# Expert blocks of a four-layer attention and feed-forward kernel: gathers placed ahead of accumulating stores, first gathers and weights issued during routing, router logits in four column tiles of 32

## The reference

```
x = x + cross_attention_0(layernorm(x), ctx)
x = x + moe_0(layernorm(x))            # 8 experts, top 2, F = 704
x = x + feature_map_attention_1(ctx, ctx, layernorm(x))
x = x + block_1(layernorm(x))          # latent attention, then MoE: 7 experts of F = 256 and a shared one
x = x + nearest_context_row(layernorm(x), ctx)
x = x + fp4_feed_forward_2(layernorm(x))
x = x + cross_attention_3(layernorm(x), ctx)
x = x + moe_3(layernorm(x))            # 8 experts, top 2, F = 512

moe: probs = softmax(x @ router_w); top 2 of 8, weights normalised
     out[token] = sum over its 2 experts of w * (silu(x @ Wg[e]) * (x @ Wu[e])) @ Wd[e]
```

## Time and profile before

| | us |
|---|---|
| median of 3 runs | 1805.71 (1800.82 to 1808.09) |
| profiled execution, its own time | 1800.69 |
| its span | 1798.8 |
| stages e0n to the first gate product of e0b | 133.2 to 188.4 |
| blocks of e0b, first to last rows turned | 187.5 to 476.0 |
| stages e3n to the first gate product of e3b | 1474.3 to 1525.5 |
| blocks of e3b, first to last rows turned | 1524.6 to 1769.9 |
| PE busy | 1550.2 (86%) |
| POOL busy | 486.0 (27%) |
| mean granted TensorE clock | 0.946 |

### The profile page before, as it was taken

The page is one execution under the profiler, slowest core; times in us unless marked ns, Lnnn a source line. Parts: engine busy times, 40 slices in busy tenths (PEclk is TensorE's granted clock), DMA queues, the critical chain, the costliest instruction groups (busy, mean ns, idle before and its releaser), DMA issues. The chain is left out here.

```text
span 1798.8 us, 33336 instructions
## 1 busy us (share of the span) xinstructions
PE 1550.2 (86%) x11830; PEld 1155.5 (64%) x11831; DVE 958.4 (53%) x2462; ACT 487.2 (27%) x1029; POOL 486.0 (27%) x594
## 2 busy tenths in 40 slices
PE   5887999999979986999979899578897888988885
PEld 3653899999858742455444566346665654878785
DVE  4455244444359866766556333689885464222221
ACT  2331111011067531455621122223322431000000
POOL 0101344444400001111102343422120102455543
PEclk9998999999969998999999999788998998999998
DMA  4108677777510017244115133200000025666665
GB/s 142 40 8 277 221 226 223 218 212 222 154 50 2 2 36 194 61 108 111 52 32 170 50 88 82 62 24 13 1 1 1 2 62 189 206 200 201 200 182 140
DMA packets 128641, 200.84 MB, mean 112 GB/s; under 512 B 20368, under 2 KB 77968, under 8 KB 128336
## 3 DMA queue, kind: packets, MB, share of 16 engines
q1 hardware_dynamic: 107696, 169.65, 29.3%
q0 software_dynamic: 20832, 29.68, 8.4%
HBM read 166.21 MB, written 35.16 MB: 112 GB/s over the span
## 5 line engine op out<-in xcount | busy, mean ns | idle before, releaser
L1528 DVE TENSOR_REDUCE l1a_nm<-l1a_sc 128x1 f32<-128x512 f32 (+3 forms) x256 | 107.1, 482 | 53.7 <-PE l1a_sc L1664 53.7
L2271 PEld LDWEIGHTS e0b_gp<-e0b_xT,e0b_wgu 128*128 128x128 f32 x936 | 110.5, 192 | 4.2 <-issue 1.5
L2271 PE MATMUL e0b_gp<-e0b_xT,e0b_wgu 128*128 128x128 f32 x936 | 111.0, 275 | 1.9 <-DVE e0b_hT L2350 1.4
L2331 ACT ACTIVATE e0b_sg<-e0b_gp 128x640 f32<-128x640 f32 x78 | 33.5, 481 | 270.9 <-PE e0b_gp L2271 270.9
L2242 POOL DMA_INDIRECT y_sum<-e0b_yb,e_token x39 | 63.5, 1628 | 145.6 <-DVE e0b_yb L2358 142.5
L2271 PE MATMUL e0b_up<-e0b_xT,e0b_wgu 128*128 128x128 f32 x780 | 93.5, 275 | 0.0
L2242 POOL DMA_INDIRECT y_sum<-e3b_yb,e_token x39 | 63.0, 1617 | 102.2 <-DVE e3b_yb L2358 99.3
L2271 PEld LDWEIGHTS e0b_up<-e0b_xT,e0b_wgu 128*128 128x128 f32 x780 | 90.2, 192 | 0.0
L2331 ACT ACTIVATE e3b_sg<-e3b_gp 128x512 f32<-128x512 f32 x39 | 23.3, 597 | 236.2 <-PE e3b_gp L2271 236.2
L2271 PE MATMUL e3b_up<-e3b_xT,e3b_wgu 128*128 128x128 f32 x624 | 80.3, 285 | 0.0
L2271 PEld LDWEIGHTS e3b_gp<-e3b_xT,e3b_wgu 128*128 128x128 f32 x624 | 75.6, 192 | 3.5 <-issue 0.9
(11 more groups left out here) (619 smaller groups left out, 3755.9 us busy)
## 6 DMA issues: line engine op xcount, KB each, us to landing
e3b_wgu<-in_L_ffn_W SPq DMA_DIRECT2D x78, 512.0 KB, 4.6
e0b_wgu<-in_L_ffn_gate_proj SPq DMA_DIRECT2D x39, 704.0 KB, 4.3
e0b_wgu<-in_L_ffn_up_proj SPq DMA_DIRECT2D x39, 704.0 KB, 5.6
x_rows<-xn SPq DMA_DIRECT2D x3, 2048.0 KB, 8.6
l_parts<-l1p_split SPq DMA_DIRECT2D x16, 384.0 KB, 3.1
l_stack_k<-l_parts SPq DMA_DIRECT2D x48, 128.0 KB, 2.7
l_stack_q<-l_parts SPq DMA_DIRECT2D x48, 128.0 KB, 3.0
y_slots<-e1b_yb SPq DMA_DIRECT2D x38, 128.0 KB
```

Source lines behind the costliest of these rows:

```text
L1528: nc.vector.tensor_reduce(nm[:, g % 2, q, i:i + 1], sc[q], AX_X, ALU.max, negate=True).then_inc(max_done, 1)
L2271: last = nc.tensor.matmul(dst[:, f, :], wgu[j][:, k, at + f * P:at + (f + 1) * P], xT[j][:, k, :], start=(k == 0), stop=(k == KC - 1))
L2331: last = nc.scalar.activation(sg[rows, chunks, :], gp[rows, chunks, :], ACT.Silu)
```

## The change

It moves instructions on POOL, SP, PE, ACT and DVE and adds few.

1. **POOL's order in blocks**: `send` and `fetch_weight` stand one block later, behind `fetch(n)`: `send(n - 4)`, `fetch_weight(n - 2)`.
2. **Issued during route** (e0, e3): gathers of blocks 0 and 1 (POOL, at the end of route, once `token` is made) and the gate and up weights of block 0 (SP, once `owner` is made). The dummy matmuls at the opening of blocks go from 30 to 4; 16 are added at the end of route.
3. **Memory of the down projections in e0**: the last pieces (those with the half-filled chunk that POOL must clear) now go to `xnT`, so the clearing waits for nothing; the others go to `xn`, once its store has landed.
4. **Router logits**: the router columns are padded with zeros to 32; each of the four token tiles of a batch is made in a column tile of its own (32 stationary columns, 128 moving), so `lt` is 128 by 128, and one transpose turns a batch.
5. **a1**: four groups of four tiles; the first group's statistics stand ahead of the value bias additions on DVE; one Sqrt and one Exp table load fewer.

```diff
@@ normalise @@
-                lt = [st.enter_context(nc.psum_tensor(f"{tag}_lt{j}", [E, S], F32)) for j in range(2)]
-                lts = st.enter_context(nc.sbuf_tensor(f"{tag}_lts", [E, B, S], F32))
+                lt = [st.enter_context(nc.psum_tensor(f"{tag}_lt{j}", [P, P], F32)) for j in range(2)]
+                lts = st.enter_context(nc.sbuf_tensor(f"{tag}_lts", [P, B, P], F32))
...
                         for k in range(KC):
-                            last = nc.tensor.matmul(lt[b % 2][:], wr[:, k, :], xnT[:, k, b * S:(b + 1) * S],
-                                                    start=(k == 0), stop=(k == KC - 1))
+                            for t in range(TB):
+                                at = (b * TB + t) * P
+                                last = nc.tensor.matmul(lt[b % 2][t * ROUTER:(t + 1) * ROUTER, :], wr[:, k, :], xnT[:, k, at:at + P],
+                                                        start=(k == 0), stop=(k == KC - 1))
...
                         pe.wait_ge(lt_copied, b + 1)
-                        for t in range(TB):
-                            nc.tensor.transpose(lp[:, b * TB + t, 0:E], lts[:, b, t * P:(t + 1) * P], ident[0:E, 0:E])
+                        nc.tensor.transpose(lp[:, b * TB:(b + 1) * TB, :].rearrange("p t e -> p (t e)"), lts[:, b, :], ident)
@@ feature_attention @@
-        GROUPS = [(0, 2), (2, 4)] + [(b * TB, (b + 1) * TB) for b in range(1, B)]
+        GROUPS = [(b * TB, (b + 1) * TB) for b in range(B)]
...
                     copy_rows(0)
-                    roots(1)
                     act.preload_act_table(ACT.Exp)
@@ SummedBlocks @@
-            homes = [inner, xnT, xn]
+            homes = [inner, xn, xnT] if self.FC > 4 else [inner, xnT]
...
+        def load_gate_up(self, sp, owner, n, j):
+            e = sp.value_load(owner[0:1, bass.ds(n, 1)], min_val=0, max_val=self.E - 1)
+            for at, m in ((0, self.w_gate), (self.F, self.w_up)):
+                sp.dma_start(self.wgu[j][:, :, at:at + self.F], m[e].rearrange("(k p) f -> p k f", p=P)).then_inc(self.gu_in[j], 16)
@@ route @@
                     last.then_inc(token_made, 1)
+                    if plan is not None:
+                        stay_busy(idle[:], 16)
...
                     if plan is not None:
-                        for dst, source in plan.late[0]:
+                        if plan.LEFT:
+                            sp.dma_start(x_rows[T * P:, :].rearrange("(t p) d -> p t d", p=P), xn[:, 0:2, :]).then_inc(sent, 16)
+                            sp.wait_ge(left_cleared, 1)
+                        for dst, source in plan.late[-1]:
                             sp.dma_start(dst, source).then_inc(plan.kept, 16)
-                        if len(plan.late) > 1:
-                            sp.dma_start(x_rows[T * P:, :].rearrange("(t p) d -> p t d", p=P), xn[:, 0:2, :]).then_inc(sent, 16)
+                        sp.wait_ge(step, 20)
+                        plan.load_gate_up(sp, owner, 0, 0)
+                        if plan.LEFT:
                             sp.wait_ge(sent, 32)
-                            sp.wait_ge(left_cleared, 1)
-                            for dst, source in plan.late[1]:
+                            for dst, source in plan.late[0]:
                                 sp.dma_start(dst, source).then_inc(plan.kept, 16)
...
                     if plan is not None and plan.LEFT:
-                        pool.wait_ge(sent, 32)
                         plan.clear_left(left_cleared)
...
+                    if plan is not None:
+                        pool.wait_ge(routed, 2)
+                        pool.wait_ge(sent, 32 if plan.LEFT else 16)
+                        for n in range(2):
+                            pool.indirect_dma_start(plan.xb[n][:], None, x_rows, bass.IndirectOffsetOnAxis(ap=token[:, n:n + 1], axis=0))\
+                                .then_inc(rows_in[n], 16)
@@ blocks @@
-                    load_gate_up(0, 0)
-                    load_gate_up(1, 1)
+                    plan.load_gate_up(sp, owner, 1, 1)
...
-                    fetch(0)
-                    fetch(1)
                     fetch_weight(0)
                     fetch_weight(1)
                     pool.wait_ge(plan.start_written, 16 * len(plan.start))
                     for n in range(2, NB):
                         fetch(n)
-                        if n >= 3:
-                            send(n - 3)
-                            fetch_weight(n - 1)
-                    send(NB - 3)
-                    fetch_weight(NB - 1)
-                    send(NB - 2)
-                    send(NB - 1)
+                        if n >= 4:
+                            send(n - 4)
+                            fetch_weight(n - 2)
+                    for n in range(NB - 4, NB):
+                        send(n)
+                        if n + 2 < NB:
+                            fetch_weight(n + 2)
...
-                    stay_busy(gp[:, 0:4, :].rearrange("p f c -> p (f c)"), 30)
+                    stay_busy(gp[:, 0:4, :].rearrange("p f c -> p (f c)"), 4)
```

More of the change, by code:

```diff
@@ L262, in _ @@
                     sp.dma_start(dst, src).then_inc(weights_loaded[0], 16)
+            @block.gpsimd
+            def _(pool):
+                for router in w.router:
+                    nc.gpsimd.memset(router[:], 0.0).then_inc(cleared, 1)
+                pool.wait_ge(cleared, len(w.router))
             @block.vector
@@ L856, in _ @@
                     split_bias()
-                    for b in range(B):
+                    for t in range(TB):
+                        count(t)
+                    for t in range(TB):
+                        aggregate(t)
+                    for b in range(2):
                         dve.wait_ge(v_made, b // 2 * 2 + 2)
```

77 lines of the change are left out of this document (39 added, 38 removed).

## The result

| | before | changed |
|---|---|---|
| median, us | 1803.26 (1799.31 to 1808.09, 4 runs) | 1744.36 (1742.65 to 1747.71, 4 runs) |
| changed / before | | 0.9677, 95% interval 0.965 to 0.9704 |
| profiled execution: time, span, mean granted clock | 1800.7, 1798.8, 0.946 | 1747.71, 1745.8, 0.944 |

The forecast was 1739, range 1724 to 1757. The kernel is 58.9 us faster by the medians; 63.9 were forecast.

What follows compares the result with a forecast made beforehand. PE, busy 86% of the span, was taken as the bound, so only its waits could give much. Terms 35.5 + 6.6 + 4.8 + 10 + 4.5 + 2.5 = 63.9 us, from 1800.7 to 1736.8; median taken as 1739, range 1724 to 1757.

Steps and rivals of the forecast that it cites:

- main term: In e3b, POOL's new order removes PE's waits for gathers: 6.46 to 5.52 us a block, 35.5 us in all.
- The logits: In e3n and e1n, a batch's router logits take 0.53 us in column tiles: 6.6 and 4.8 us earlier ends.
- e3r to e3b: From routing to e3b's first gate product, early gathers and weights give 4.5 us; ends 3 and 5.5.
- a1: At a1's opening, one table load fewer before queries(0) and earlier statistics give 2.5 us; ends 0 and 7.
- e0n to e0b: From e0n to e0b's first gate product: gate(0) at 178.1 instead of 188.42, 10 us; ends 6 and 11.
- the clearing no longer waits, so e0r goes as e3r did: In e0r, PE reaches its inverting matmuls 19.3 us after the stage's start, at 168.2.
- at 347 GB/s that is 8.7 us, 175 to 177. So blocks start at 176.5: At e0r's end, SP's queue drains its remaining 3.0 MB in 8.7 us, so e0b's blocks start at 176.5.
- Weights: Rival: in e3b, block weights become PE's wait and 12 us are lost, giving 1750 us; chance 0.12.
- The tiles: Rival: the router logits' column tiles don't overlap, a batch still costs 1.95 us, giving 1749 us; chance 0.08.
- The gathers: Rival: in e3b, gathers stay late, limited by landing, and a block keeps 6.46 us, giving 1774 us; chance 0.05.
- The chain of stores: Rival: in e3b, stores waiting for the previous landing stop POOL's queue, making the kernel slower, 1815 us; chance 0.02.
- More than forecast: Rival: a1's opening keeps the upper clock (7 instead of 2.5 us) and e0 reaches 11: 1731 us; chance 0.12.

Runs made afterwards that it cites:

- e1: Kernel before with only POOL's new order in both summed expert stages: 1766.37 us against 1804.86, ratio 0.9796.
- e2: Changed kernel with POOL's old order put back (store n-3 and row weights n-1 behind the gather of n): 1781.58 us, ratio 0.9863.
- e4: Changed kernel with the router logits as before (two matmuls of 512 columns, 16 small transposes a batch): 1761.63 us, ratio 0.9765.
- e7: Changed kernel with a1's opening as before (statistics in groups of two tiles, second root ahead of queries(0), value biases first): 1746.78 us, ratio 0.9681.
- e3: As a run, not the stage: changed kernel with the store of w_pairs issued ahead of the late down-weight loads: 1743.97 us, ratio 0.9668.
- e9: On top of e3's edit, the 2.7 MB of f2w_rows loaded in e0b behind block 1's weights instead of in e0n: 1739.18 us, ratio 0.965.
- e5: Changed kernel with 36 dummy products instead of 16 at the end of e0r alone: 1743.76 us, ratio 0.9662.
- e6: Changed kernel with first gathers and gate/up weights issued in the blocks' stage, 30 dummies at its start, none ending routing: 1747.26 us, ratio 0.9691.
- e10: On top of e3's edit, the first two gathers issued in the blocks' own stage again: 1753.51 us, ratio 0.9729.

## Why the prediction was right, and where it was not

**Sign, size and main term: right.** e3b was to lose its waits and go from 6.46 to 5.52 us a block. It went to 5.44, and e1 and e2 show that POOL's order does this alone. The measured 38.5 lies above both ends, 30.5 (waits only) and 35.5 (waits and clock): the pace of 5.52 came from one pair of products of the kernel before, and 0.08 us less in 38 blocks is the 3 us. Much of that is the one trace: over the twelve traces with the new order (the changed kernel and all runs but e2) e3b's span was 206.8 to 210.6 us, which is 34.7 to 38.5 us less than before, and the changed kernel's is at the low end. Some 35 us would do for the term as well.

**The logits: right.** "I take 0.53" for a batch; measured 0.57. e3n gained 5.6 for 6.6 and e1n 4.0 for 4.8. e4 gives 10 to 11 us for the two directly.

**e3r to e3b and a1: right** within their ends: 5.0 for 4.5, and 3.4 for 2.5, of which e7 confirms 2.4. Two errors of e3r's working hid each other: the gathers landed in 2.8 us (e3) and not in the 5.2 taken, and the stage waited for the second of them, where only the first was counted.

**e0n to e0b: wrong, 10 us forecast, 4.2 at gate(0) and 1.4 at the end of e0b,** under the lower end of 6 that I had given. Three steps of it failed, in the order of their place:

- "the clearing no longer waits, so e0r goes as e3r did". PE stood idle for 3.79 us before e0r, since SP's loads outlast its work in e0n, and its 20 dummies took 6.14 us and not 4.48. It came to the inverting matmuls 20.4 us after the stage's start, not 19.3. In e9, without that idle time, the 1 us is back: 145.00 to 164.24. That they started at 168.38, next to the 168.2 forecast, is luck: the stage began 0.9 us before the 148.9 I had taken.
- "at 347 GB/s that is 8.7 us, 175 to 177. So blocks start at 176.5". The bytes and their rate were right: from 168.5 to 177 the engines moved the 3.0 MB at 355 GB/s. The step that failed is the one from there to the stage's end: I took the time at which the queue has moved its bytes for the time at which its last transfers have landed. `w_pairs` landed at 179.8, 2.8 us later, and the stage ended at 180. What makes this tail wasn't tried. And I had not seen at all that the gathers hold the stage's end by themselves until they land, 5.7 us after issue in e3.
- gate(0) was put at its old duration. Nothing in the working asked what PE does between its 16 dummies and the stage's end. It stands idle for 5.5 us and comes back at the lower clock, 2.5 us for the first product alone (e5). A stage whose end is set by a queue needs its dummies counted against the queue, not against PE's own work.

On the Trainium skill's rule ("DMA: Bandwidth & Descriptors", section "Issuing engines are not separate DMA queues") I had allowed half a us. The trace bears the rule out: within one run the gathers took 5.7 us among SP's loads and 2.8 where there were none. The price was more than I gave it, since it fell on a stage's end: by e6 the whole early part gives e0 nothing, where it brings e3 3.7 us.

**The rivals.** Weights did not become e3b's bound: PE waited 0.2 us once near its end. The tiles do overlap. The gathers did not stay late: their waits are gone. The chain of stores held POOL 4.9 us in two pieces in e3b and nobody else. "More than forecast" rested on a1 and e0; neither came.

**The scatter.** I had taken the profiled execution as 5.0 us under the median and put that down partly to e3b's waiting. The changed kernel has no such waits and scatters by 5.1 us still. Between the traces of before and after, the difference sits in stages that the change leaves alone, at products that run at the lower clock in one of the two.

## What to carry to other kernels

When one queue carries loads, stores and gathers in a fixed order, ask for each entry when it is needed and what stands in front of it: moving each gather ahead of a store that waits for the end of an iteration took out all 30 us of waits and their clock losses, with no instruction added or removed. Ahead of a barrier count to the last landing that something waits for, POOL's gathers of the stage included, and not to the time at which the bytes have moved; here 2.8 us lay between the two. And see that PE is kept busy to the barrier and not only to the end of its work. And where one delay hides behind another of the same length, taking out one shows nothing: e3 looked like a failed theory until e10 took out the second too.
